# A two-layer decoder of attention and experts: where a planned attention step places the pieces of other batches

## What is computed

```python
x = _layernorm(x + _L0_attn_ref(x, ...), axis=-1)
x = _layernorm(x + _L0_xattn_ref(x, ctx_768, ...), axis=-1)
x = _layernorm(x + _L0_ffn_ref(x, ...), axis=-1)
x = _layernorm(x + _L1_attn_ref(x, ...), axis=-1)
x = _layernorm(x + _L1_xattn_ref(x, ctx_768, ...), axis=-1)
x = _layernorm(x + _L1_ffn_ref(x, ...), axis=-1)
```

## Time and profile before

| | |
|---|---|
| median of 3 runs | 2742.83 us (2741.75 to 2742.94) |
| the profiled execution | 2762.94 us |
| its span, first to last instruction | 2761.2 us |
| mean granted clock of PE in it | 0.952 |
| PE busy | 2504.2 us |
| VectorE, ScalarE, POOL busy | 1496.9, 1315.6, 455.4 us |

### The profile page before, as it was taken

The page is one execution under the profiler, slowest core; times in us unless marked ns, Lnnn a source line. Parts: engine busy times, 40 slices in busy tenths (PEclk is TensorE's granted clock), DMA queues, the critical chain, the costliest instruction groups (busy, mean ns, idle before and its releaser), DMA issues. The chain is left out here.

```text
span 2761.2 us, 47077 instructions
## 1 busy us (share of the span) xinstructions
PE 2504.2 (91%) x15751; PEld 1439.7 (52%) x15752; DVE 1496.9 (54%) x4204; ACT 1315.6 (48%) x2826; POOL 455.4 (16%) x735
## 2 busy tenths in 40 slices
PE   5999999999979889999699999999998988599991
PEld 3555544444434456676365654444445555366761
DVE  2555777789744600013455598878756664322224
ACT  2655466677754521212255557766675543122220
POOL 4233212101100000000113322022122122110004
PEclk8999999999999999999799999999999987799995
DMA  7544534232800022203755443342322554121003
GB/s 222 160 142 142 144 100 107 54 85 58 267 1 1 1 98 67 95 12 115 201 151 142 140 115 85 81 107 62 109 77 81 165 165 148 52 63 34 31 31 97
DMA packets 156894, 276.76 MB, mean 100 GB/s; under 512 B 22928, under 2 KB 98960, under 8 KB 152208
## 3 DMA queue, kind: packets, MB, share of 16 engines
q1 hardware_dynamic: 152896, 262.56, 33.2%
q0 software_dynamic: 3792, 11.54, 1.3%
HBM read 195.51 MB, written 95.29 MB: 105 GB/s over the span
## 5 line engine op out<-in xcount | busy, mean ns | idle before, releaser
L1635 ACT ACTIVATE second_p<-psum 128x512 f32<-128x512 f32 (+3 forms) x1024 | 460.2, 524 | 248.7 <-PE psum L1436 233.4
L1635 ACT ACTIVATE first_p<-psum 128x512 f32<-128x512 f32 (+3 forms) x768 | 364.9, 551 | 150.1 <-PE psum L1436 146.8
L1733 DVE TENSOR_REDUCE second_max_parts<-psum 128x1 f32<-128x512 f32 x512 | 324.9, 685 | 54.6 <-PE psum L1413 44.5
L1733 DVE TENSOR_REDUCE first_max_parts<-psum 128x1 f32<-128x512 f32 x512 | 324.9, 685 | 52.0 <-PE psum L1413 42.7
L1729 DVE CUSTOM_DVE_ANT_0 second_masked<-psum,mask_qk 128x384 f32<-128x384 f32 (+3 forms) x512 | 229.7, 489 | 185.7 <-PE psum L1413 159.5
L1448 PE MATMUL psum<-second_p,second_v_aug 128*32 128x512 f32 (+3 forms) x2048 | 237.1, 535 | 0.5 <-ACT second_o_sum L1642 0.4
L1413 PE MATMUL psum<-second_k,second_q 64*128 64x512 f32 (+3 forms) x1024 | 211.9, 413 | 24.3 <-DMA second_k<-a_k_parts 11.4
L1426 PE MATMUL psum<-second_q,second_k 64*128 64x512 f32 (+3 forms) x1024 | 215.1, 416 | 5.8 <-DVE second_max_parts L1729 4.5
L1436 PE MATMUL psum<-second_shift_T,choose 64*128 64x512 f32 (+3 forms) x1024 | 198.3, 382 | 0.0
L1448 PE MATMUL psum<-first_p,first_v_aug 128*32 128x512 f32 (+3 forms) x1536 | 185.9, 556 | 1.2 <-ACT first_p L1635 0.7
L2512 ACT ACTIVATE routed_space<-psum,routed_bias 128x128 f32<-128x128 f32 x312 | 84.7, 382 | 213.3 <-PE psum L2437 213.3
(11 more groups left out here) (341 smaller groups left out, 3865.4 us busy)
## 6 DMA issues: line engine op xcount, KB each, us to landing
first_k<-c_k_parts SPq DMA_DIRECT2D x64, 256.0 KB, 4.7
second_q<-a_q_parts SPq DMA_DIRECT2D x128, 128.0 KB, 3.0
second_k<-a_k_parts SPq DMA_DIRECT2D x128, 128.0 KB, 3.0
second_k<-c_k_parts SPq DMA_DIRECT2D x64, 256.0 KB, 4.7
first_q<-a_q_parts SPq DMA_DIRECT2D x64, 128.0 KB, 3.2
first_k<-a_k_parts SPq DMA_DIRECT2D x64, 128.0 KB, 3.2
c_k_parts<-first_held SPq DMA_DIRECT2D x16, 512.0 KB, 3.1
first_q<-c_q_parts SPq DMA_DIRECT2D x64, 128.0 KB, 4.2
```

The source lines that it names most:

```text
L1635: evacuated(act.activation(probs[tile % 2][:, 2 * h + p, q0:SEQ], bank[:, q0:SEQ], ACT.Exp, scale=scale), event)
L1733: evacuated(v.reduce_max(max_parts[n % 2][:, h, p, qt, k0 // BANK:k0 // BANK + 1], bank[:, 0:width], axis=AX_X), event)
```

## The change

One call moves. The share of a step's own pieces is taken directly behind that step's values (and, in step 0, behind the drain of the group before), and no longer at the step's end. How many pieces a step gets stays the same.

```diff
                 plan.append(("values", n, t - 1))
             elif n:
                 plan.extend([("values", n - 1, layer_of(n - 1).key_tiles - 1), ("drain", n - 1, 0)])
+            share(own, t + 1, steps)
             if t == 1:
                 if n:
                     plan.append(("turn", n - 1, 0))
...
             share(units, 2 * t + 2, 2 * steps)
             if n + 1 < groups and t < 3:
                 plan.extend([("chain", n + 1, 2 * t), ("chain", n + 1, 2 * t + 1)])
-            share(own, t + 1, steps)
         assert not units and not own
```

## The result

The changed kernel takes 2802.62 us (median of 4 runs, 2794.86 to 2815.97), the kernel before beside it 2742.48 us: ratio 1.0225, 95% interval 1.0185 to 1.0264, +60 us. Forecast were 2783, with a range of 2755 to 2815 and 0.90 for slower. Sign and range hold, but the result lies 20 us above the forecast, 6 us above its own range of 2772 to 2797, and where rival 2 (clock falls) had put its number.

A forecast was written before the change was run, and what follows sets the result against it. The prediction took PE to bound the kernel, busy 2504 of 2761 us. Its terms summed to +40.0 us, which on the median of 2742.83 us gave 2783 us, 1.5% slower, with a range of 2755 to 2815.

The forecast's parts named there:

- rival 2: The clock falls where new waits reach 2 us and at a few more places: 2802 us, chance 0.15.
- step 0: Causal groups' first step: exponentials come late for the values, +9.8 us over 28 steps, plus +2.4 us for 10 splits.
- step 1: Causal groups: 0.15 us each for 26 steps and 0.4 once in group 0, +4.2 us.
- step 2: Causal groups: a split delays ScalarE's exponentials, 0.35 us for each of 11 splits, +3.9 us.
- step 3: Causal groups: the next group's first scores wait for the shift's copy, late behind the piece, +6.8 us.
- SP's queue: Loads at step 1 go out behind the piece's store; units wait 2.0 us in five groups, +9.5 us.
- groups 14 and 15: These run at VectorE's pace and the piece parts its reductions unevenly: −6 to +8, taken as +2 us.
- cross groups: The second unit's reductions queue behind VectorE's part of the piece; with gains taken off, +2.4 us.
- last gate groups: Around them −1 us: VectorE's block of step 3 in group 35 meets one unit less.
- the two gains that didn't come: In cross groups, PE's smoother passage into some 53 pieces, −4.8 us, and splits whose ScalarE part begins earlier, −2.0 us.
- The clock: Left out of the sum: causal waits of 0.2 to 0.6 us, and output waits of 1.3 us, leave no fall.

The follow-up runs named there:

- e3: The changed kernel with the loads of step 1 ahead of the piece again: 2788.6 us, ratio 1.0166.
- e12: The kernel before, with causal groups' chain operations and then the piece between scores 1 and the second unit: 2755.5 us, ratio 1.0037.
- e2: The kernel before, with the piece directly behind the values only in cross groups and the last two groups of a stage: 2761.5 us, ratio 1.0066.
- e7: The changed kernel with loads first; where pieces begin with an attention output's turn, only the turn stands behind the values, the rest at step's end: 2773.1 us.
- e10: The kernel before, with the loads and value load of step 1 moved behind that step's pieces: 2805.9 us, ratio 1.0227.
- e6: The kernel before, with the piece of causal groups between scores 1 and the second unit: 2783.8 us, ratio 1.0152.

## Why the prediction was right, and where it missed

The terms, as measured in the traces of the changed kernel and e3 (no term twice):

| term | forecast | measured |
|---|---|---|
| step 0, exponentials uncovered | +12.2 | +8.8 |
| step 1 | +4.2 | +1.0 |
| step 2 | +3.9 | +3.8 |
| step 3 | +6.8 | +8.7 |
| SP's queue, falls behind it included | +9.5 | +14 |
| falls in the output product's step | 0 | +5 |
| groups 14 and 15 | +2 | +2.5 |
| cross groups | +2.4 | +16 to +18 |
| last gate groups, stalls left out | −1 | about 0 |

The sum is 60 to 62.

- *Step 0.* The mechanism held row by row: splits +0.57 (0.35 and 0.24 forecast), input turns +0.47 or 0.29, values +0.29. An output product shows almost none (+0.06), and in the last gate groups, +0.1 to 0.3, there was less to lose.
- *Step 1* was mis-sized: +0.04 a step, not 0.15. I put that down to the turn behind the piece, which covers the exponentials; no run isolates it.
- *Step 2.* +0.42 for eleven splits (0.35 forecast); values −0.08.
- *Step 3.* Behind a split +0.70 (0.73 forecast), behind a values piece +0.04 (0.17), behind an output product −0.2 to +0.9. The +0.70 is the right size, but the trace doesn't show my reason for it alone. In group 4 of the first stage PE's wait is put down to the unit's maxima, late behind the piece (done at 160.52), and the shift's copy is done at 160.47, so the two end within 0.05 us of each other:

```profile
160.53 0.51 PE L1426 MATMUL psum<-first_q,first_k 64*128 64x512 f32 x2 [0.74 <-DVE first_max_parts L1729]
```
```profile
159.88 0.59 ACT L1646 ACTIVATE first_shift_T<-psum 128x512 fp32r<-128x512 f32 x1
```
```profile
160.44 0.08 DVE L1729 DVE_READ_ACCUMULATOR2_ANT first_max_parts<- 128x1 f32 x1
```

What I had not is a step 3 *without* a piece behind a split in step 2: six times +0.66, PE waiting 0.36 for the shift rows. That the chain's operations beside the tail cause it is argued: with the chain ahead of the piece (e12) the same steps grow by 0.19 only.
- *SP's queue.* The right five groups and the right waits (1.3 to 2.2 in four of them, 0.5 in one; 2.0 forecast), without the falls behind them. In group 8 of the first stage, step 0 lasts 6.08 instead of 4.67 at full clock.
- *Cross groups* are the step that failed. Forecast +2.4, measured +16 to +18. Of the 13 us missing in e2's trace, 8 are the two gains that didn't come (−6.8 forecast, about +1 in the steps), 3 the steps of the input rows (nearly all of it the clock, see above), 5 the steps with long chain operations; output chains and slot rows came 3 under. I had asked what waits in each engine's queue behind the moved piece and not what it runs *beside*: in the earlier trace rows the tail of 1.28 us was before my eyes as a time on SP's path only.
- *The clock.* Left out of the sum, rightly for the single waits of 0.3 to 0.4 us a step, wrongly for the longer. The prediction misread the trace of the kernel before twice: output waits of 1.3 us do leave a fall there (group 45, above), and so do waits of 0.51, 0.60 and 0.19 us in a row in causal group 14, with a granted clock of 0.65 in the 4.8 us behind them (step 0: 8.39 us, 6.75 in e2). Rival 2 gave it 19 us; the falls are more than it had and smaller: in the changed kernel those of the first stage cost 1.4 to 1.6 us each, two of the second 1.8 and 2.4, not 2.7. Stretch by stretch, the causal groups of the first stage before and after:

```profile
88.00:320.00 232.00, 226.15 (x1856) 135.13 (x1855) 131.75 (x550) 130.15 (x302) 68.41 (x103) 0.99 0.50 143
```
```profile
88.00:345.00 257.00, 236.58 (x1869) 143.39 (x1868) 146.26 (x556) 130.15 (x305) 69.63 (x105) 0.97 0.42 128
```

So the result is rival 2's number, but not by its mechanism alone: the falls in causal groups make some 10 us of the surplus, the cross groups 13, and smaller terms came under. The range holds because it took in rival 2; the cross groups' 13 us were in no rival, and that they fit too, with the causal steps 5 us under, is luck. The Trainium skill's rule of micro-idles that I weighed (TensorE: Matmul & The Clock Gate, "A second HAM failure mode: psum-queue depth-cycling") isn't borne out for single short waits by e3 and e7 (granted clock 1.00 behind a series of 0.3 to 0.4 us); group 14 of the kernel before, with several in a row, agrees with it.

## What to carry to other kernels

- Work between a producer's feed and its consumer is cover. Before you move it, write down who uses it as cover, on PE and on every queue that it passes: here loads that go out 5 to 11 us later on SP's queue alone (e10) were worth 2.3%, and the last 1.0 us of it turned waits of 0.5 to 2.2 us into 3.2 to 3.8.
- When an engine's busy time grows with the same instructions, look at its shortest operations first, and at what GpSimd does in the same microsecond.
- Move the first half of a pair, not the whole: the turn forward and the product left in place gave 13 us, the whole piece forward took 60.

## What the runs showed of the hardware

A VectorE operation on 128x16 in SBUF (0.20 us) that meets a GpSimd addition of two SBUF tiles stands until that addition is done: 1.18 us beside a tail of 1.26, 1.11 beside one of 1.28, 1.22 to 1.41 beside the addition of 1.28 in cross groups, 0.67 beside the one of 0.72 in causal groups. In the changed kernel's trace 74 chain operations start inside such an addition, and every one ends 0.03 to 0.07 us behind it. Of VectorE's operations that read PSUM (L1729, L1733), 165 start inside one, and 142 end more than 0.2 us away from its end. The row's length shows it as busy time, not as a wait. The Trainium skill (SBUF — State Buffer, "SBUF: two separate sides") says that the port pair which VectorE and GpSimd share is an exclusive lock, and that the loser is blocked for the whole instruction; the rows here agree, for casts and for operations with two SBUF inputs. It took e6 to make me read it.
